# Key stores waited for among the first experts, side arrays of the third attention issued by ScalarE with part of the common terms added by matmul products, and single last third tiles

## The reference

```python
x = x + L0_xattn(layernorm(x), ctx, ctx, mask, Wq, Wk, Wv, Wo)   # first attention, masked scores
x = x + L0_ffn(layernorm(x), ...)        # second attention, then one of 4 experts (width 1024) per row
x = x + L1_xattn(layernorm(x), ctx, ctx, fside, fside, pad, am)  # third attention
x = x + L1_ffn(layernorm(x), ...)        # two of 16 experts (width 512) per row, and two shared ones
# third attention, b and h over 4 x 16:
scores = einsum('bhtd,bhsd->bhts', q, k) * scale
scores = scores + am[None, None]         # one (512, 512) array, fside_SxS2_0
scores = where(pad, -inf, scores)
scores = scores + fside + fside          # (4, 16, 512, 512), added twice
out = einsum('bhts,bhsd->bhtd', softmax(scores), v)
```

## Time and profile before

| what | us |
|---|---|
| runs shown | 1677.45, 1681.86, 1683.98; median 1681.86 |
| profiled execution, its time | 1682.88 |
| its span | 1681.1 |
| PE, DVE, ACT, POOL busy | 1526.3, 1068.9, 839.3, 531.1 |
| POOL's M = C - M, 63 of 64 | 286.1 |
| mean granted clock | 0.965 |

### The profile page before, as it was taken

How to read it: one execution, slowest core, us unless ns; L and a number is a source line. 1 busy time by engine, 2 the same in 40 slices (tenths; PEclk the granted TensorE clock), 3 DMA queues, 4 the chain that set the end, 5 groups by cost and what they waited for, 6 DMA issues and landing times. The chain is left out here.

```text
span 1681.1 us, 24349 instructions
## 1 busy us (share of the span) xinstructions
PE 1526.3 (91%) x8288; PEld 1020.1 (61%) x8288; DVE 1068.9 (64%) x2656; ACT 839.3 (50%) x1341; POOL 531.1 (32%) x348
## 2 busy tenths in 40 slices
PE   7899999979999997779966789899979999999996
PEld 4566666655655455469953555555554666777774
DVE  5699999854888776636647888888866451222221
ACT  3688888825566663312215777778733222111110
POOL 0112110003000000301112999999713227133323
PEclk9999999989999999879987999999999999999998
DMA  7433422106334314467737888898532002244541
GB/s 255 164 126 107 137 89 64 38 10 228 96 106 111 103 55 157 150 210 243 260 116 263 298 292 307 288 310 292 174 133 94 1 4 96 85 140 144 142 145 12
DMA packets 135559, 254.02 MB, mean 151 GB/s; under 512 B 29724, under 2 KB 67505, under 8 KB 126097
## 3 DMA queue, kind: packets, MB, share of 16 engines
q1 hardware_dynamic: 124256, 241.11, 43.6%
q0 software_dynamic: 10128, 10.35, 2.3%
q10 hardware_dynamic: 1056, 1.05, 0.2%
HBM read 202.69 MB, written 54.39 MB: 153 GB/s over the span
## 5 line engine op out<-in xcount | busy, mean ns | idle before, releaser
L667 DVE CUSTOM_DVE_ANT_0 X<-pS,M 128x512 f32<-128x512 f32 x512 | 340.5, 690 | 59.5 <-POOL M L594 38.4
L617 PE MATMUL pT<-ident,X 128*128 128x128 f32 x2048 | 305.5, 272 | 2.8 <-ACT PT L705 2.8
L608 PE MATMUL pS<-k,q 65*128 65x512 f32 (+1 forms) x512 | 254.4, 497 | 45.3 <-DVE mx L667 31.9
L594 POOL TENSOR_TENSOR M<-C,M 128x2048 f32<-128x2048 f32 x63 | 286.1, 4591 | 5.3 <-DMA M<-in_fside_Bx16xSxS 4.8
L617 PEld LDWEIGHTS pT<-ident,X 128*128 128x128 f32 x2048 | 253.9, 140 | 42.5 <-ACT X L695 3.8
L608 PEld LDWEIGHTS pS<-k,q 65*128 65x128 f32 (+1 forms) x512 | 98.0, 191 | 163.8 <-DVE mx L667 100.3
L468 PE MATMUL pO<-PT,V 128*17 128x512 f32 x1536 | 194.6, 597 | 0.0
L865 DVE TENSOR_REDUCE nm<-pS 128x1 fp32r<-128x512 f32 x256 | 161.2, 684 | 38.9 <-PE pS L838 32.8
L695 ACT ACTIVATE X<-X,nm 128x512 f32<-128x512 f32 x256 | 164.0, 712 | 24.9 <-POOL nm L576 24.6
L695 ACT ACTIVATE X<-X,mx 128x512 f32<-128x512 f32 x256 | 165.1, 715 | 3.8 <-DVE mx L667 3.4
L679 DVE COPY PT<-pT 128x1024 f32<-128x1024 f32 x128 | 156.2, 1220 | 6.7 <-PE pT L617 6.7
(11 more groups left out here) (321 smaller groups left out, 2254.6 us busy)
## 6 DMA issues: line engine op xcount, KB each, us to landing
M<-in_fside_Bx16xSxS SPq DMA_DIRECT2D x64, 1024.0 KB, 7.2
w<-in_L_ffn_ew SPq DMA_DIRECT2D x48, 512.0 KB, 5.2
w<-in_L_ffn_W SPq DMA_DIRECT2D x23, 1024.0 KB, 5.4
q<-q_stacks SPq DMA_DIRECT2D x192, 64.0 KB, 3.7
k<-k_stacks SPq DMA_DIRECT2D x128, 64.0 KB, 2.9
k_stacks<-hi SPq DMA_DIRECT2D x24, 256.0 KB, 2.4
q_stacks<-hi SPq DMA_DIRECT2D x24, 256.0 KB, 2.1
q_stacks<-lo SPq DMA_DIRECT2D x24, 256.0 KB, 2.1
```

Of the source, the lines that this page charges most:

```text
L594: eng.tensor_tensor(M[:, slot], C[:, b % 2], M[:, slot], ALU.subtract).then_inc(s_m, 1)
L608: eng.matmul(pS[:, qt % 2, :], of, by, start=True, stop=True).then_inc(s_s, 1)
L617: ins = eng.transpose(pT[:, kt, qt * P:(qt + 1) * P], X[:, t % 3, qt, kt * P:(kt + 1) * P], self.ident[:])
L667: eng.tensor_tensor_reduce(X[:, i % 3, qt, :], pS[:, qt % 2, :], M[:, slot, qt, :], 2.0 if not per_group else 1.0, HIGHEST if not per_grou ...
```

## The change

It makes six edits.

- `route_top1`: SP no longer waits for the key stores at the end; `top1_tiles` waits for them on SP before tile 4's loads. The first two row tiles are loaded by ACT.
- `queries`: POOL's subtraction for head 0 goes.
- `attention_turned` with `side`: the side array of head h + 4 is loaded by ACT after the exps of head h, no longer by SP.
- For all four tiles of head 0 and for tile 0 of each head i with i % 3 = 2 (`multiplied`, 25 tiles), PE adds C to the scores by a product ident x C into the same bank. For these POOL leaves the tile of M as loaded, DVE computes X = 2 (M - pS) with its row maximum, and ACT negates the maximum and waits for it before the exp.
- C's reload waits for one subtraction fewer.
- `experts`: for experts 14 and 15 the third tile is computed and scattered for each expert alone; the rest of 14 is scattered before the tiles of 15, with half the rows.

```diff
+MULTIPLIED = 3
+            def multiplied(i):
+                if per_group:
+                    return 0
+                return ST if i == 0 else int(i % MULTIPLIED == MULTIPLIED - 1)
...
-                    def load_bias(n):
-                        need(eng, s_x, 4 * (n - slots + 1))
-                        eng.dma_start(M[:, n % slots], side[n]).then_inc(s_f[n % slots], 16)
-                        if not per_group and i + slots < NBH:
-                            load_bias(i + slots)
...
-                        for i in range(READY, NBH):
+                        for i in range(1, NBH):
...
-                            eng.tensor_tensor(M[:, slot], C[:, b % 2], M[:, slot], ALU.subtract).then_inc(s_m, 1)
+                            first = multiplied(i)
+                            eng.tensor_tensor(M[:, slot, first:ST], C[:, b % 2, first:ST], M[:, slot, first:ST], ALU.subtract).then_inc(s_m, 1)
...
-                        eng.matmul(pS[:, qt % 2, :], of, by, start=True, stop=True).then_inc(s_s, 1)
+                        more = qt < multiplied(i)
+                        ins = eng.matmul(pS[:, qt % 2, :], of, by, start=True, stop=not more)
+                        if more:
+                            b = i // H
+                            eng.wait_ge(s_c[b % 2], 16 * (b // 2 + 1))
+                            ins = eng.matmul(pS[:, qt % 2, :], self.ident[:], C[:, b % 2, qt, :], start=False, stop=True)
+                        ins.then_inc(s_s, 1)
...
+                                if qt < multiplied(i):
+                                    eng.tensor_tensor_reduce(X[:, i % 3, qt, :], M[:, slot, qt, :], pS[:, qt % 2, :], 2.0, LOWEST, ALU.subtract, ALU.max,
+                                                             mx[:, i % 3, qt:qt + 1]).then_inc(s_x, 1)
+                                    continue
...
+                                if qt < multiplied(h):
+                                    eng.activation(nm[:, h % 3, qt:qt + 1], mx[:, h % 3, qt:qt + 1], ACT.Copy, scale=-1.0).then_inc(s_nm, 1)
+                                    eng.wait_ge(s_nm, negated[h] + qt + 1)
+                                    eng.activation(X[:, h % 3, qt, :], X[:, h % 3, qt, :], ACT.Exp, bias=nm[:, h % 3, qt:qt + 1]).then_inc(s_p, 1)
+                                    continue
...
+                            n = h + slots
+                            if not per_group and n < NBH:
+                                eng.dma_start(M[:, n % slots], side[n]).then_inc(s_f[n % slots], 16)
...
-                    eng.wait_ge(s_ks, 16 * 2 * NK)
...
                         if i == 4:
+                            eng.wait_ge(self.s_ks, 16 * 2 * B * KD)
...
+                    for i in range(2):
+                        eng.dma_start(xs[:, i, :], XS[i * P:(i + 1) * P, :]).then_inc(s_xs[i], 16)
...
-                    eng.wait_ge(s_lo, NQ)
-                    eng.wait_ge(self.s_c[0], 16)
-                    for n in range(READY):
-                        eng.wait_ge(self.s_f[n], 16)
-                        eng.tensor_tensor(self.M[:, n], self.C[:, 0], self.M[:, n], ALU.subtract).then_inc(self.s_m, 1)
...
+            def alone(i):
+                return i >= E1 - 2
...
-                        if i % 2 == 1:
+                        if i % 2 == 1 or alone(i):
...
-                                for part, e in enumerate((i - 1, i)):
+                                for part, e in ([(i % 2, i)] if alone(i) else enumerate((i - 1, i))):
...
+                            if alone(i):
+                                eng.wait_ge(s_st3, 32 * pair + 16)
...
+                        if alone(i):
+                            eng.wait_ge(s_yb, first_tile(i) + 3)
+                            scatter_third(i, i % 2)
```

More of the change, by code:

```diff
@@ L39 @@
 FILL = 192
-READY = 1
+MULTIPLIED = 3
 BLANK = 4
@@ L516, in bias_of @@
                 return (i // H % 2, 0) if per_group else (i % slots, i // slots)
+            def multiplied(i):
+                if per_group:
+                    return 0
+                return ST if i == 0 else int(i % MULTIPLIED == MULTIPLIED - 1)
+            negated = [sum(multiplied(i) for i in range(h)) for h in range(NBH)]
             if rows is not None:
@@ L532, in write_blank @@
                                           blank[:, c % 2]).then_inc(s_bl[c % 2], 16)
-                    def load_bias(n):
-                        need(eng, s_x, 4 * (n - slots + 1))
-                        eng.dma_start(M[:, n % slots], side[n]).then_inc(s_f[n % slots], 16)
                     def load_common(b):
-                        need(eng, s_m, H * (b - 1))
+                        need(eng, s_m, H * (b - 1) - 1)
                         eng.dma_start(C[:, b % 2], common[b]).then_inc(s_c[b % 2], 16)
@@ L661, in _ @@
                                     need(eng, s_bm, ST * (i // H))
+                            elif i == 0:
+                                eng.wait_ge(s_f[slot], 16)
                             else:
-                                eng.wait_ge(s_m, i + 1)
+                                eng.wait_ge(s_m, i)
                             need(eng, s_t, 2 * (i - 2))
@@ L1059, in route_top1 @@
             pv = self.ps("pv", [P, 2, 512], ctx)
-            s_pk, s_pv, s_ke, s_ve, s_hi, s_lo, s_ks = (self.sem(n, ctx) for n in ("s_pk", "s_pv", "s_ke", "s_ve", "s_hi", "s_lo", "s_ks"))
+            s_pk, s_pv, s_ke, s_ve, s_hi, s_lo = (self.sem(n, ctx) for n in ("s_pk", "s_pv", "s_ke", "s_ve", "s_hi", "s_lo"))
+            s_ks = self.s_ks = self.sem("s_ks")
             key, kf, gt = (self.sb(n, [P, NT], ctx=ctx) for n in ("key", "kf", "gt"))
@@ L1290, in _ @@
                             eng.wait_ge(s_st[i % 2], (i // 2 - 1) * 16)
-                        eng.dma_start(xs[:, i % 4, :], XS[i * P:(i + 1) * P, :]).then_inc(s_xs[i % 4], 16)
+                        if i >= 2:
+                            eng.dma_start(xs[:, i % 4, :], XS[i * P:(i + 1) * P, :]).then_inc(s_xs[i % 4], 16)
                     eng.wait_ge(s_cs, 16 * B)
@@ L2039, in experts @@
             LOADS = (3 + len(CAP_TILES) + 1) * 16
+            def alone(i):
+                return i >= E1 - 2
             def first_tile(i):
-                return i // 2 * 5 + i % 2 * 2
+                return i // 2 * 5 + i % 2 * (3 if alone(i) else 2)
             def tiles(i):
-                return [first_tile(i) + j for j in range(2 + i % 2)]
+                return [first_tile(i) + j for j in range(2 + (1 if alone(i) else i % 2))]
             with nc.Block() as block:
@@ L2138, in scatter_third @@
                     def scatter_third(i, part):
-                        scatter(third_id[:, i // 2 % 2, 2 * part:2 * part + 1], y3[:, i // 2 % 2, :], s_st3)
+                        rows = slice(0, P // 2) if part == 0 else slice(0, P)
+                        scatter(third_id[rows, i // 2 % 2, 2 * part:2 * part + 1], y3[rows, i // 2 % 2, :], s_st3)
                     eng.wait_ge(s_out, 16 * B)
@@ L2150, in _ @@
                             scatter(xs[:, i % 4, j, D:ROW], ys[:, i % 2, j, :], s_st[i % 2])
-                        if i % 2 == 1:
+                        if alone(i):
+                            eng.wait_ge(s_yb, first_tile(i) + 3)
+                            scatter_third(i, i % 2)
+                        elif i % 2 == 1:
                             eng.wait_ge(s_yb, first_tile(i) + 3)
@@ L2156, in _ @@
                             scatter_third(i, 0)
+                    eng.wait_ge(s_st[1], 32 * (E1 // 2))
                     eng.wait_ge(s_st3, 32 * (E1 // 2))
@@ L2184, in _ @@
                                     need(eng, s_st3, 32 * (a // 2 - 1))
+                                if j == 2 and alone(a):
+                                    rows = slice(a % 2 * (P // 2), (a % 2 + 1) * (P // 2))
+                                    eng.tensor_scalar(y3[rows, a // 2 % 2, :], py[rows, n % 2, 0:D], third_id[rows, a // 2 % 2, 1:2], None,
+                                                      ALU.mult).then_inc(s_yb, 1)
+                                    continue
                                 if j < 2:
```

2 lines of the change are left out of this document (1 added, 1 removed).

## The result

The changed kernel is slower. In eight runs each on one chip it takes 1695.62 us (median, 1689.22 to 1699.71), the kernel before 1683.06 (1677.45 to 1686.13): a ratio of 1.0073, 95% interval 1.0058 to 1.0088. The forecast was 1670, a gain. The profiled execution took 1696.65 us for a span of 1694.6, 13.5 more than before.

A forecast was written before the change was run, and what follows sets the result against it. POOL's subtractions were taken to bound the third attention, PE next. Gains of 8.7 us there, 0.4 at the first and 2.6 at the last experts, 11.7 in all, gave about 1670 us; range 1665 to 1675, 8 in 10 1662 to 1680.

The forecast's parts named there:

- Stalls by loads: Third attention, heads 1 to 63: late q and k loads cost 1.6 us of stalls, bounds 0 and 6.
- Heads 1 to 63 without loads: Third attention: 62 heads at 4.14 us plus 18.1 us for 21 products of 0.86, 274.8 against 286.3 us.
- rival 4: Third attention: half of each product hides, 9 us more are gained, 1661 us; chance 0.10.
- POOL no longer the bound: Third attention: POOL's 57.75 subtractions of 4.59 us take 265 us, 4.2 a head, far under 275.
- a sign of error: Third attention: the forecast is wrong if POOL still waits for M loads in many heads.
- The start: Third attention's start: 3.8 us sooner, head 0's four products cost 5.0 (bounds 3.4 and 6.9); net 1.2 us later.
- ScalarE: Third attention: ACT's head with a 0.54 us load issue is 4.37 us against a pace of 4.43; costed at nothing.
- The lower bound: ACT in the third attention: no cost even with a longer issue, if it runs while the last exp is in the engine.
- rivals 1 and 3: Third attention: ACT's issues held by SP's, 1680 (middle 1677), chance 0.14; or each issue holds ACT, about 1693, chance 0.07.
- rival 3: Third attention: each load issue holds ACT, at 1.0 us an issue 4.83 a head; slower, about 1693 us; chance 0.07.
- rival 2: Third attention: side loads bind, M landing after 9.5 us, 4.55 a head; 1676 and up to 1680 us; chance 0.09.
- Experts: First experts gain 0.4 us (bounds 0 and 0.5); last experts gain 2.6 (bounds 1.5 and 3.4), expert 14's tile costing 1.73.

The follow-up runs named there:

- the run of both expert edits: The kernel before with only key stores awaited later, two row tiles loaded by ACT, and single last third tiles; ratio 0.9976.

## Why the prediction was wrong

**The step that failed** is "I leave 1.6 us of stalls; bounds 0 and 6", under "Stalls by loads". The mechanism had been named beside it ("the same bytes pass") and then read the wrong way: I took the DMA share of 0.84 as room. The runs show in its place: with a quarter of M's bytes the heads take 269.5 us, with all of them 302.3, so the stalls by loads are 32.8 us for 1.6, of which a third key buffer alone gives back 22.7. The forecast looked at the mean share and at the M landing; a wait on ten small loads is set by when the last of them lands, and its slack was 9 us for 7.7. I moved a queue's large loads and asked only when they would land themselves, not whose place they would take.

The Trainium skill (DMA: Bandwidth & Descriptors, Queues, rings and completion order) says that each DMA engine takes turns, packet by packet, between the queues that have work. The landing times fit it (a small load takes at least 2.9 us beside M on the other queue, 1.9 before), but the run with M ahead on one queue shows that the order within a queue matters as well. The turns themselves no run here shows.

**Heads 1 to 63 without loads.** Forecast 62 x 4.14 + 18.1 = 274.8. Measured, with a quarter of M's bytes, 269.5: 4.12 a head, right, and 0.68 a product for 0.86, as far as one pair of executions tells. By them rival 4 (half hidden) was right by a fifth of each product, 3.8 us, but it had no say as long as loads were late.

**POOL no longer the bound.** Right for its work: 41 whole subtractions of 4.575 us and 20 of 3.483. (The 265 us are 4.27 a head, not 4.2.) That it waits for loads in many heads was named as a sign of error, and it does, 43.5 us; but the sign was badly chosen. An engine that is no longer the bound has idle time, and something must end it: DVE waited for POOL's M 2.4 us in all. The error lay with k, for which no sign was named.

**The start.** SP drained at 912.7, POOL long before, and PE began at 913.73, 5.1 us sooner: 3.8 by POOL's drain of 4.60, which is gone; 1.3 had been gained before that stage. From there to head 1's first X 8.25 us, forecast 9.35. Two products ran at half clock (1.91 and 1.81 with their records' overlap), two at full, as forecast. From one tile's scores to the next it was 2.58 and 2.36 us at the half clock, 1.32 and 1.31 at the full one, and 0.86 without a product at the half clock, in the run of both expert edits: at full clock the rest of a tile shrinks too, and that gave back 1.1 more than I took off. Counted from SP's drain, head 1's first X comes 9.3 us later for 9.2: net 0.1, forecast 1.2, inside the bounds.

**ScalarE.** An issue is 0.34 us, not 0.54, and runs beside the exps. The lower bound held, rivals 1 and 3 have no row that bears them out. By the Trainium skill's rule on the shared descriptor generator (Perfetto Trace Analysis, DMA Instruction — HWDGE (DVE, Sync)) issues would be held; here ACT's were not, while SP's ten took 5.91 us for 5.14. With a quarter of M's bytes, and the same 60 issues on ACT, SP's ten took 5.27: most of what they lost goes with the bytes, and at most 0.13 is left for the rule. The sign came out as in rival 3, for another reason: the 0.07 for slower priced only ACT's time. No rival had the loads of k late.

**M late (rival 2).** M was not issued 1 to 2 us behind its X but 0.05, and landed after 6.0 us, sooner than before: 0.05 + 6.0 + 4.6 = 10.7 us for the 13.3 that I added up. The pace that rival 2 was to set, 4.55, is not the one that came (4.88).

**Experts.** At the routing's end 0.4 forecast; POOL's drain now ends the block, at 722.3, and from its start to the next block's first transposes it is 3.7 us (720.9 to 724.62) for 4.1 (722.0 to 726.06). In the last experts the lone third tile took 1.87 us (forecast 1.73); from the last down products to POOL's drain it is 10.2 us for 14.3 (1662.56 to 1676.9), and the drain stayed at 3.98: a gain of 4.2 - 1.9 = 2.3, forecast 2.6. The run of both edits alone gave 4 us, with 3.0 in its interval.

**The sum, mended:** 1681.1 - 1.2 - 1.3 + (302.3 - 286.3) = 1694.6. The 1.2 and 1.3 are what the two profiled executions show, with the differences between executions in them.

## What to carry to other kernels

Before a large load goes to another queue, list the small loads that it was in order with, and their slack: here a DMA share of 0.85 had no room for loads with 1 to 2 us to spare. Give the small ones a further buffer first; here 2 KB per partition brought the heads from 302.3 to 279.6 us. When the work of the bounding engine is cut, check that its loads come as fast as its new pace: with M on SP's queue POOL's work fell and its waits for M grew nearly as much. And read a wait by who waits behind it: POOL's 43.5 us for M made DVE wait 2.4 us in the changed kernel, PE's 40.5 for k went with the loss of which the third key buffer gave back 22.7.

## What the runs showed of the hardware

- One 1 MB load per head on a second queue lengthened the landing of ten small loads (512 KB together) from 7.7 to 10.9 us; the same load ahead of them in their own queue, to 9.3.
- From 930 to 1180 us the DMA engines moved 299 GB/s at a busy share of 0.86 (M on SP behind the pair's loads), 309 at 0.93 and 305 at 1.01: a share near 1 did not mean more bytes than one of 0.93.
- Load issues on ACT's queue took 0.34 us, ran beside its computations in 60 of 60 cases, and started 1.0 us (median) before the last of the four exps that stand ahead of it in the program.
- The granted clock fell to 0.50 for 3.4 to 6.8 us seven times in the heads of the run with M issued by ACT alone, each time in or just behind a wait of PE of 1.9 to 3.5 us; in the kernel before it stayed at 1.00 in the heads.
- Eight records on half of the output rows took 1.87 us, sixteen on both halves 1.88: the second half had cost nothing.
